# Mamba layer: projection and 3x3 convolution in four channel groups, with the image kept channel by row on chip

## What is computed

```python
zxbcdt = einsum('bchw,oc->bohw', norm(x), in_proj_w)   # 844 outputs: gate 384, conv channels 448, dt 12
xbc    = silu(depthwise_conv3x3(conv_channels, conv_w) + conv_b)     # 448 channels, SAME padding
dt     = softplus(dt_raw + dt_bias)
# then, row by row of the image: chunked scan over 128 pixels, norm, gate, out_proj_w, + x
```

## Time and profile before

| | us |
|---|---|
| median of 3 runs | 3409.54 (3408.66 to 3413.07) |
| profiled execution, own time | 3413.66 |
| its span in the trace | 3411.6 |

### The profile page before, as it was taken

One profiled execution on the slowest core, in us unless ns is written; L12 is line 12 of the kernel. 1 busy time (PEld: TensorE's weight loads), 2 busy tenths in 40 slices (PEclk: granted clock), 3 DMA queues, 4 the chain that ended last, 5 costly groups with the idle time before them and its releaser, 6 DMA issues. The chain is left out here.

```text
span 3411.6 us, 68799 instructions
## 1 busy us (share of the span) xinstructions
PE 3089.8 (91%) x22716; PEld 2368.3 (69%) x22716; DVE 1888.3 (55%) x3431; ACT 1478.2 (43%) x3945; POOL 1141.5 (33%) x1355
## 2 busy tenths in 40 slices
PE   0888979899999999499999999999999698869888
PEld 0656434499999999388888888888888565536564
DVE  4444722344444444467676777767767544463447
ACT  1344412122222222366666666666666244424444
POOL 1321410000000000366565666666656421143114
PEclk9999989899999999589898998989989899989999
DMA  8414844200404020211111111111111413593148
GB/s 212 117 25 83 269 128 140 81 1 7 166 5 169 0 87 0 108 41 45 40 45 42 44 47 41 45 45 45 45 40 45 119 54 52 109 302 87 33 79 277
DMA packets 203641, 283.38 MB, mean 83 GB/s; under 512 B 81915, under 2 KB 141447, under 8 KB 195623
## 3 DMA queue, kind: packets, MB, share of 16 engines
q1 hardware_dynamic: 185018, 230.99, 24.8%
q10 hardware_dynamic: 13998, 45.63, 3.4%
q0 software_dynamic: 4496, 4.98, 0.9%
HBM read 163.86 MB, written 95.74 MB: 76 GB/s over the span
## 5 line engine op out<-in xcount | busy, mean ns | idle before, releaser
L427 PE MATMUL l_conv_conv<-l_image,l_arena 128*128 (+1 forms) x2688 | 612.4, 397 | 0.0
L427 PEld LDWEIGHTS l_conv_conv<-l_image,l_arena 128*128 128x128 f32 x2688 | 541.0, 205 | 28.7
L440 DVE COPY l_arena<-l_conv_gen 128x384 f32<-128x384 f32 x448 | 321.8, 830 | 361.0 <-PE l_conv_gen L413 361.0
L1543 ACT ACTIVATE l_scan_decay<-l_scan_cum,l_scan_row_scalars 128x128 f32<-128x128 f32 x1536 | 429.3, 392 | 136.5 <-PE l_scan_cum L1442 136.4
L1460 PE MATMUL l_scan_y_intra<-l_scan_xdt,l_scan_att 128*128 128x32 f32 x3072 | 416.8, 282 | 1.9 <-DVE l_scan_att L1575 1.9
L1575 DVE TENSOR_TENSOR l_scan_att<-l_scan_decay,l_scan_causal_scores 128x512 f32<-128x512 f32 x384 | 348.9, 935 | 119.3 <-ACT l_scan_decay L1549 118.9
L1460 PEld LDWEIGHTS l_scan_y_intra<-l_scan_xdt,l_scan_att 128*128 128x128 f32 x3072 | 410.9, 208 | 4.1 <-issue 4.1
L1124 ACT ACTIVATE l_image<-l_conv_conv,l_conv_bias 128x128 f32 (+1 forms) x448 | 143.0, 468 | 494.4 <-PE l_conv_conv L427 474.0
L797 ACT COPY l_arena<-l_body_bank 128x384 f32<-128x384 f32 x192 | 148.9, 881 | 321.4 <-PE l_body_bank L680 321.4
L1515 PEld LDWEIGHTS l_scan_projected<-l_scan_yz,l_scan_wo 128*96 128x96 f32 x1536 | 210.8, 194 | 103.2 <-issue 102.0
L1185 POOL MEMSET l_steps_parts<- 128x8192 bf16 x1 | 6.9, 6927 | 707.7 <-POOLq L74 707.7
(11 more groups left out here) (172 smaller groups left out, 5096.8 us busy)
## 6 DMA issues: line engine op xcount, KB each, us to landing
convolved_rows<-l_image ACTq DMA_DIRECT2D x32, 896.0 KB, 10.3
l_scan_xc<-convolved_rows SPq DMA_DIRECT2D x128, 224.0 KB, 2.8
x_after<-l_arena SPq DMA_DIRECT2D x64, 384.0 KB, 5.0
l_arena<-x_after SPq DMA_DIRECT2D x64, 384.0 KB, 5.9
l_arena<-x_after SPq DMA_DIRECT2D x16, 1024.0 KB, 6.8
l_arena<-l_arena SPq DMA_DIRECT2D x72, 210.4 KB
projected_rows<-l_arena ACTq DMA_DIRECT2D x32, 448.0 KB, 2.6
l_image<-projected_rows SPq DMA_DIRECT2D x16, 896.0 KB, 11.9
```

The costliest lines, as they stand in the source:

```text
L427: last = nc.tensor.matmul(self.out[q][:, c, :], self.mats[:, b, a * CC + 4 * q + c, :], image[:, a:a + self.rows, bass.ds(c0 + 4 * q + c, ...
L440: copy(self.mats[:, b, :, f * OPB:(f + 1) * OPB].rearrange("p c o -> p o c"), self.gen[f % 4][:])\
L1543: nc.scalar.activation(decay[:, b % 2, 4 * g + h, :], cum[(b + g) % 2][:, h, :], ACT.Relu, scale=-1.0, bias=rs[:, b, CUM, 4 * g + h:4 * g ...
```

## The change

`fold_norm` now folds only the 384 gate columns, and also puts mean and scale by channel into `scales`. `project_rows`, `convolve_rows` and `Bands` are replaced by one phase, `convolve_image`. For each of four groups of 112 channels it first projects the whole image in 16 units of 8 rows and then convolves 7 chunks. x is loaded for every group anew (four times 12.6 MB), normalized in place by DVE (channels 0 to 127) and POOL (128 to 191), and multiplied by the unfolded weights `wx`: for each row one matmul of height 128 and one of height 64. DVE and ACT copy a unit from PSUM into `image`, now `[w, channel, row]`. The convolution streams `image[:, ch, a:a+H]`, which is contiguous. The PSUM banks are 4 for the projection, 2 for `gen` (before 4), 2 for the convolution (before 4). Of the matrix copies DVE makes three of four, ACT the fourth. Silu writes to a tile of its own, `staged`, and SP, not ACT, issues the stores. The DRAM tensor `proj` is gone. The instruction streams are unrolled.

```diff
@@ fold_norm
+                dve.wait_ge(gathered, 1)
+                nc.vector.tensor_copy(scales[:], pt[:]).then_inc(scales_step, 1)
...
+                for t in range(2):
+                    for n, per_channel in enumerate((mv[:, :, 0], var)):
+                        for kk in range(2):
+                            last = nc.tensor.matmul(pt[:, t, n:n + 1], gather[:, t, kk, :], per_channel[:, kk:kk + 1],
+                                                    start=(kk == 0), stop=(kk == 1))
...
-class Bands:
-def project_rows(nc, name, x, wf, arena, images, dt_raw, proj, H):
-def convolve_rows(nc, name, table, taps, bias_dram, arena, image, proj, xbc, last_stored, H):
+def convolve_image(nc, name, flat, wx, scales, table, taps, bias_dram, dt_bias, arena, image, staged, xs, dt_raw, xbc, H):
+        proj = [ph.ps(f"proj{j}", [128, BANK]) for j in range(4)]
+        gen = [ph.ps(f"gen{j}", [128, OPB, 3 * CC]) for j in range(2)]
+        conv = [ph.ps(f"conv{j}", [128, 4, H]) for j in range(2)]
...
+                def load(u):
+                    if u >= 2:
+                        sp.wait_ge(projected, 2 * (u - 1))
+                    for tile, source in loads(u):
+                        sp.dma_start(tile, source).then_inc(x_landed[u % 2], 16)
...
+                    if g + 1 < 4:
+                        load((g + 1) * units)
+                        load((g + 1) * units + 1)
+                    sp.wait_ge(activated, GROUP * (g + 1))
+                    for q in range(8):
+                        rows = slice(q * H // 8, (q + 1) * H // 8)
+                        sp.dma_start(xbc[g, :, rows, :], staged[:, rows, :]).then_inc(stored, 16)
...
+                for u in range(4 * units):
+                    pool.wait_ge(x_landed[u % 2], 64 * (u // 2 + 1))
+                    nc.gpsimd.tensor_scalar(rest[:, u % 2], rest[:, u % 2], scales[:, 1, 0:1], scales[:, 1, 1:2], ALU.subtract, ALU.mult)\
+                        .then_inc(rest_normed, 1)
...
+                def build(s, f):
+                    n = s * fills + f
+                    if n >= 2:
+                        wait_copied(pe, n - 2)
...
+                def project(g, u):
+                    b = u % 2
+                    width, at = columns(g), first(g)
+                    pe.wait_ge(normed, 2 * (u + 1))
+                    pe.wait_ge(rest_normed, u + 1)
+                    if u >= 2:
+                        for s in range(2):
+                            pe.wait_ge(kept[s], u - 1)
+                        pe.wait_ge(dt_kept, 2 * min(u - 1, units))
+                    for s in range(2):
+                        for r in range(XR):
+                            nc.tensor.matmul(proj[2 * b + s][:, r * width:(r + 1) * width], main[:, b, s, r * W:(r + 1) * W],
+                                             wx[:, 0, at:at + width], start=(r == 0), stop=False)
+                    for r in range(XR):
+                        for s in range(2):
+                            last = nc.tensor.matmul(proj[2 * b + s][:, r * width:(r + 1) * width],
+                                                    rest[64 * s:64 * (s + 1), b, r * W:(r + 1) * W],
+                                                    wx[64 * s:64 * (s + 1), 1, at:at + width], start=False, stop=(r == XR - 1))
+                            if r == XR - 1:
+                                last.then_inc(projected, 1)
+
...
+                    for c in range(4):
+                        ch = s % chunks * CC + 4 * q + c
+                        for a in range(3):
+                            last = nc.tensor.matmul(conv[n % 2][:, c, :], mats[:, s % 2, a * CC + 4 * q + c, :],
+                                                    image[:, ch, a:a + H], start=(a == 0), stop=(a == 2))
...
+            def copy_matrices(eng, copy, copied, s, f):
+                n = s * fills + f
+                if s >= 2:
+                    eng.wait_ge(convolved, 4 * (s - 1))
+                eng.wait_ge(built, n + 1)
+                copy(mats[:, s % 2, :, f * OPB:(f + 1) * OPB].rearrange("p c o -> p o c"), gen[n % 2][:]).then_inc(copied, 1)
+
+            def keep(eng, copy, g, u, s):
+                if g > 0:
+                    eng.wait_ge(convolved, 4 * chunks * g)
+                eng.wait_ge(projected, 2 * u + s + 1)
+                h = (u % units * 2 + s) * XR
+                copy(image[:, :, 1 + h:1 + h + XR].rearrange("p c r -> p r c"),
+                     proj[2 * (u % 2) + s][:, 0:XR * columns(g)].rearrange("p (r c) -> p r c", r=XR)[:, :, 0:GROUP]).then_inc(kept[s], 1)
...
+                    for u in range(g * units, (g + 1) * units):
+                        keep(dve, nc.vector.tensor_copy, g, u, 1)
...
+                        if u + 2 < 4 * units:
+                            norm(u + 2)
+                    for t in range(chunks):
+                        s = g * chunks + t
+                        if s + 1 < 4 * chunks:
+                            for f in range(fills):
+                                if f % 4 < 3:
...
+                    if g > 0:
+                        act.wait_ge(stored, 8 * 16 * g)
...
+                                nc.scalar.activation(staged[:, :, ch], conv[n % 2][:, c, :], ACT.Silu,
+                                                     bias=bias[:, g * GROUP + ch:g * GROUP + ch + 1]).then_inc(activated, 1)
```

More of the change, by code:

```diff
@@ L262, in _ @@
             def _(pool):
[L263 to L264 removed]
+                nc.gpsimd.memset(half[:], -0.5).then_inc(half_set, 1)
                 for tile, source in rounding:
                     nc.gpsimd.dma_start(tile, source).then_inc(rounded, 16)
+                pool.wait_ge(half_set, 1)
+                pool.wait_ge(scales_step, 2)
+                nc.gpsimd.tensor_tensor(scales[:, :, 1], scales[:, :, 1], half[:], ALU.pow).then_inc(scales_step, 1)
                 if rounding:
@@ L289, in _ @@
                 dve.wait_ge(zero, 1)
-                dve.wait_ge(landed, 16 if extra is None else 32)
+                dve.wait_ge(landed, 16)
                 for k in range(2):
@@ new lines, in _ @@
+                load(0)
+                sp.dma_start(bias[:], bias_dram).then_inc(bias_landed, 16)
+                load(1)
+                for g in range(4):
+                    for u in range(g * units + 2, (g + 1) * units):
+                        load(u)
+                    if g + 1 < 4:
[5 more added lines that the diff above has]
+                        sp.dma_start(xbc[g, :, rows, :], staged[:, rows, :]).then_inc(stored, 16)
@@ L1000, in _ @@
             @block.tensor
             def _(pe):
-                pe.wait_ge(ones, 1)
-                with pe.Fori(0, slabs // 2) as i:
-                    for b in range(2):
-                        pe.wait_ge(landed[b], i * 16 + 16)
-                        for r in range(SLAB):
-                            pe.wait_ge(copied[r % 2], (i * 2 + b) * (SLAB // 2) + r // 2 + 1)
-                            for k in range(2):
-                                rows = CH + 1 - k
-                                last = nc.tensor.matmul(banks[r % 8][:], xt[0:rows, b, k, r, :], wf[0:rows, k, D_INNER:D_INNER + O],
-                                                        start=(k == 0), stop=(k == 1))
-                            last.then_inc(filled, 1)
-                        pe.wait_ge(filled, (i * 2 + b) * SLAB + SLAB)
-                        pe.sem_inc(used[b], 1)
```

333 lines of the change are left out of this document (133 added, 200 removed).

## The result

The changed kernel took 3596.12 us (median of 4 runs, 3593.94 to 3599.26), the kernel before 3410.94 (4 runs, 3408.66 to 3413.07): ratio 1.0536, 95% interval 1.0511 to 1.0562. The forecast was 3453 us with a range up to 3545. The direction was right, the size was not: +185 us where +43 was forecast.

The account below looks back on a forecast made before the run. PE (TensorE) alone sets the pace, busy 91% of the span. Terms of 17 + 537 + 357 + 10 + 12 + 15 + 21 = 969 us replace 925.7, +43, giving 3453 us as median; range 3375 to 3545.

Parts of the forecast that it names:

- Convolution passes, 112 ns: Convolution: with a contiguous operand a pass takes 112 ns instead of 220, 2.60 us less per quarter, 291 us in all.
- Rival (c): Convolution: the step is not what costs 220 ns a pass; +291 us, 3744 us; chance 0.04.
- Fills on two banks, 2.18 us: Convolution: a quarter's four matrix fills wait for copies on two banks and take 2.18 us, where it was 0.82.
- Rival (d): Convolution: quarters take 5.4 us, not 4.87, because ACT or DVE copies late; +57 us, 3510 us; chance 0.10.
- TensorE in a unit, 3.5 us: Projection: a unit's 32 passes take 0.109 us each, 3.5 us, with no gain from pairing half-height passes.
- Rival (a): Projection: normalizing 1.3 us, landing 3.5, PE 3.0 as half-height pairs overlap, clock holds; 64 us less, 3389 us; chance 0.20.
- Landing, 4.0 us (3.5 to 5): Projection: a unit's four x loads, issued at 0.54 us intervals, have landed together after 4.0 us.
- Normalizing, 2.1 us (1.3 to 2.8): Projection: from landing until DVE and POOL have both normalized a unit's x takes 2.1 us.
- Clock, 0.6 us a pair: Projection: the granted clock may not hold, adding 0.6 us per pair of units, 15 us in all.
- Rival (b): Projection: the clock stays at the lower level, 7 us a unit, 14.3 a pair; +118 us, 3571 us; chance 0.13.
- Edges, 10 us: Projection to convolution: DVE normalizes the next group's first units before copying matrices, about 3 us x 3, plus 1 for the last `keep`.
- Scan and the rest: same instructions, 0: Scan and all other unchanged stages: the same instructions, so 0 us of change.

Follow-up runs that it names:

- e1_step: The changed kernel with `image` kept row by channel again, so the convolution's moving operand is read with a step of 112 elements; 3888.95 us.
- e5_gen4: The changed kernel with four banks for the matrices' fills instead of two, shared with the four of `proj`; 3445.05 us.
- e2_warm: The changed kernel with 28 bf16 matmuls, results unused, added after every second projection unit, where TensorE idles; 3543.59 us.

## Why the prediction was wrong, step by step

- **Convolution passes, 112 ns:** right, and the step is their cause (e1_step). Rival (c) is out. **Fills on two banks, 2.18 us:** right (2.2; e5_gen4). Like for like the stage took 545 for 528: 0.08 us more in each of 104 quarters (8.7 us) and the first quarters of the groups at the lower clock (8.3 us), which the forecast did not have. Rival (d), 5.4 us a quarter, is out.
- **TensorE in a unit, 3.5 us:** too high where the clock holds: units follow every 3.06 us. Two errors of opposite sign: by their starts 16 full-height passes take 1.97 us, 123 ns each and not 109, and "I give them no gain from pairing" failed, as 16 half-height passes take 1.09 us, 68 ns each. The 108 ns of the earlier trace rows were misread: those passes stream 192 columns and not 112. Full-height passes with 192 columns stand right before them in the same trace and take 1.49 us by their starts, 186 ns each, so the gain could be seen there. Rival (a) had the pairing right.

```profile
156.18 1.57 PE L676 MATMUL l_body_bank<-l_wi,l_arena 128*128 128x192 f32 x8
```

- **Landing, 4.0 us (3.5 to 5):** failed, 5.6 at the median (5.2 to 6.1). I added the issue times to the landing of a load that was alone on the queue. Here the eight loads of two units go out within 5 us and land a median 3.3 to 3.6 us after their own issue. +1.6 us a round.
- **Normalizing, 2.1 us (1.3 to 2.8):** 2.34. POOL's contiguous operation was no faster than the one in short runs (2.09): the hope in rival (a) was wrong. DVE's two operations beside it took 1.38 us together, where one took 0.54 at the median before; whether the two engines hold each other up was not tested. The Trainium skill, GPSIMD Engine Reference, "Elementwise — side-by-side cycle accounting", names about 0.77 us for 512 elements as the best case; this row is far from it.
- **Clock, 0.6 us a pair:** the largest mis-sized term of the ring. "Within the projection the clock may not hold" was written, and priced at a quarter of what it was: the wait of some 5 us lowered the clock for most of the first unit, 5.4 us where it takes 3.1, and e2_warm gave 2.1 us of it back. Rival (b) named the mechanism; it charged both units and came to 3571, nearest to the result. With the landing this makes the round 13.5 to 14.1 us for 10.7, 77 us in all. I had taken the comfort for the clock from gaps of 0.7 us; the gaps of my own forecast were 3 us, and no row showed what those do.
- **Edges, 10 us:** failed. Of the measured 29.9, 8.7 are the first fills that the forecast has under the convolution; the other 21.2 stand against 10. I had DVE's normalization in them, but not its wait for loads issued only when the last units of the group were done.
- **Stores ahead of loads, +29 us, and tail, 21 us:** mechanism and tail right (+34, of which 2 are the clock; 21.5 us).
- **First fill:** 21.4 for 17. DVE's first matrix copy begins at 458.15, behind the normalization of both first units, 10.9 us after the fold (forecast 6); the fills then take 10.4 (forecast 11). It is the same wait as at the edges.
- **"Scan and the rest: same instructions, 0":** failed by 27.6 + 3.8 us. Same instructions, TensorE always busy, yet another length, since the clock in the scan was already seen to swing. In these traces it lies between 1221 and 1253 us by what stands ahead of it, and in none under 1221, so a change ahead of the scan carried up to +30 us. That belonged in the range.

In sum +110 us on the path (projection 77, convolution 17, edges 11, first fill 4) and +31 behind it make the difference to the forecast. The range failed because its own bounds were not added: landing at 5, norms at 2.8 and the clock of rival (b) were each in the text, and all pushed one way.

## What to carry to other kernels

A ring of two buffers costs load + transform + use for every two units, and TensorE that waits can pay twice, as its next work may run at the lower clock (here 3.73 us for 2.04); ask first whether tiles that are idle in that stage can serve as more buffers. Stages that never overlap can share PSUM banks. Price the waits that a change creates with the clock that such waits leave behind, and give a long loop whose clock already swings a range of its own when anything ahead of it moves.

## What the runs showed of the hardware

- fp32 matmul, 128x128 weights, 128 columns: 112 to 115 ns a pass with contiguous columns, 218 to 221 with columns 448 bytes apart (e1_step).
- fp32 passes of half height (64 rows, in turn on partitions 0 to 63 and 64 to 127) took 68 ns each at 112 columns, where a full-height pass took 123 (16 passes in 1.09 and in 1.97 us by their starts).
- A wait of about 5 us was followed by work at half the speed: 3.73 us for the first 16 passes of a unit and 1.83 for the next 16, where the same took 2.04 and 1.15 when TensorE had just been working.
- With an empty barrier ahead of it the scan took 1251 us instead of 1221, with the same matmuls and a granted clock of 0.87 instead of 0.89 (one traced execution of each).
